# A gated cross-attention and ternary FFN block on one core: FFN tiles kept in PSUM, quads interleaved, softmax division moved

## The reference

```
x = x + tanh(g_xattn) * attention(k=ctx, v=ctx, q=layernorm(x))      # one head of 512, softmax over 722
x = x + tanh(g_ffn)   * ffn(layernorm(x))

ffn(x): h = bit_linear(x, w1)                 # 512 -> 2048
        h = depthwise_conv1d(h) along the 100 rows, 3 taps, with bias
        h = silu(h)
        return bit_linear(h, w2)              # 2048 -> 512
bit_linear(x, w): x to int8 by the row's largest |x|, w to -1, 0 or 1 by the mean of |w|
```

## Time and profile before

| | us |
|---|---|
| median of 3 runs | 380.28 (377.44 to 380.42) |
| the profiled execution, its span | 377.6 |
| PE busy | 299.4 (79%) |
| DVE busy | 213.1 (56%) |
| ACT busy | 156.3 (41%) |
| POOL busy | 99.7 (26%) |

### The profile page before, as it was taken

One profiled execution on the slowest core, in us unless ns is written; L12 is line 12 of the kernel. 1 busy time (PEld: TensorE's weight loads), 2 busy tenths in 40 slices (PEclk: granted clock), 3 DMA queues, 4 the chain that ended last, 5 costly groups with the idle time before them and its releaser, 6 DMA issues. The chain is left out here.

```text
span 377.6 us, 4595 instructions
## 1 busy us (share of the span) xinstructions
PE 299.4 (79%) x1624; PEld 216.1 (57%) x1624; DVE 213.1 (56%) x442; ACT 156.3 (41%) x291; POOL 99.7 (26%) x132
## 2 busy tenths in 40 slices
...
GB/s 202 216 228 319 39 160 259 119 0 214 10 234 146 0 104 54 112 47 1 3 117 43 102 56 0 1 2 0 23 23 0 0 1 23 0 22 0 24 0 65
DMA packets 11312, 28.02 MB, mean 74 GB/s; under 512 B 1225, under 2 KB 1225, under 8 KB 10138
## 3 DMA queue, kind: packets, MB, share of 16 engines
...
...
## 5 line engine op out<-in xcount | busy, mean ns | idle before, releaser
L861 POOL TENSOR_TENSOR z<-a,ab 128x300 f32<-128x300 f32 (+1 forms) x48 | 33.6, 700 | 72.4 <-DVE a L1088 72.4
L576 PE MATMUL pvb<-pt,ctx 120*128 120x100 f32 (+1 forms) x384 | 50.8, 294 | 1.8 <-ACT pt L747 1.8
L576 PEld LDWEIGHTS pvb<-pt,ctx 120*128 120x128 f32 (+1 forms) x384 | 49.4, 209 | 3.6 <-issue 3.5
L642 PE MATMUL ff<-xqt,w1t 128*128 128x300 bf16 (+1 forms) x192 | 35.0, 333 | 15.2 <-DVE u L1081 12.9
L555 PE MATMUL sc<-kt,qm 128*100 128x361 f32 x128 | 42.0, 478 | 0.0
L808 ACT ACTIVATE a<-u,convb,conv 128x300 f32<-128x300 f32 (+1 forms) x48 | 28.7, 598 | 17.9 <-DVE u L1081 17.9
L642 PEld LDWEIGHTS ff<-xqt,w1t 128*128 128x128 bf16 x192 | 20.0, 115 | 28.1 <-DVE u L1081 20.1
L872 POOL TENSOR_SCALAR zq<-z_i 128x300 bf16<-128x300 int8 (+1 forms) x48 | 25.9, 567 | 36.2 <-DVE z_i L1126 36.2
L536 PE MATMUL tr<-ident,ctx 120*128 120x120 f32 (+1 forms) x192 | 31.0, 285 | 2.6 <-ACT kt L726 2.2
L1088 DVE SCALAR_TENSOR_TENSOR a<-u,conv,a 128x297 f32<-128x297 f32 (+1 forms) x48 | 27.6, 574 | 8.9 <-ACT a L808 8.3
L555 PEld LDWEIGHTS sc<-kt,qm 128*100 128x100 f32 x128 | 21.3, 172 | 15.7 <-issue 1.4
...
## 6 DMA issues: line engine op xcount, KB each, us to landing
...
```

The source lines that it names most:

```text
L576: mm = nc.tensor.matmul(pvb[:, k * S:(k + 1) * S], cx[b % NCTX][0:r, i, k * P:(k + 1) * P], pt[0:r, i, :], start=(i == 0), stop=(i == 5))
L642: mm = nc.tensor.matmul(ffb[j % 2][:, 0:w], w1t[:, k, j * P:(j + 1) * P], xqt[:, k, 0:w], start=(k == 0), stop=(k == DK - 1))
L861: nc.gpsimd.tensor_tensor(z[:, j - 1, 0:w].rearrange("p (b s) -> p b s", b=nb), a1[:, n % NBUF, 0:w].rearrange("p (b s) -> p b s", b=nb), ...
```

## The change

It has three parts. First, u goes back into the tile's own PSUM bank, the `u` buffers are gone, ACT and y1 read the bank, and PE's claim of the bank waits for y1 (`y1_ok`), where it waited for u (`u_ok`). y1 now waits for `ab` too. POOL adds in place in `a1`, and silu reads `a1`. Second, silu writes `z` as [quad, column, tile of the quad], so that the four values which the maximum compares lie side by side. `quant` takes a quad at once on DVE and on POOL (4 steps, where there were 16), and `f2` waits for quads. Third, the probabilities are no longer divided: `norm` makes a [100x1] product of reciprocal and gate, and `res` multiplies y by it. `pt` no longer waits for `norm`. `FILL_CUTS` is adapted to the fewer quant steps.

```diff
@@ -66,7 +66,7 @@
 OUT_LAG = 3
 KT_LATE = 2
-FILL_CUTS = [28, 36, 50, 67, 88, 105, 117, 134]
+FILL_CUTS = [28, 36, 50, 67, 76, 93, 104, 122]
 def allowed(step, out, since):
...
@@ -131,7 +131,7 @@
         return out + [("rbc", g), ("xqt", g, b1 - 1)]
     def qz(g):
-        return [("am1", g), ("am2", g)] + [("quant", g, j) for j in range(NJ)]
+        return [("am1", g), ("am2", g)] + [("quant", g, q) for q in range(NQ)]
     def ff_f2(g, bs):
...
@@ -265,20 +265,20 @@
-        z_i8 = at(o_at + 9600 + D * 4 + 2 * NJ * GW, "z_i8", [P, NI8, GW], I8)
+        z_i8 = at(o_at + 9600 + D * 4 + 2 * NJ * GW, "z_i8", [P, 2, GW, QUAD], I8)
-        z_at = region(max(z_bytes + (3 * NBUF + 4) * t_bytes + 4 * NBUF * GW // S + 16, CHUNK * CW * 4 + CW))
-        z = at(z_at, "z", [P, NJ, GW], F32)
-        u = at(z_at + z_bytes, "u", [P, NBUF, GW], F32)
+        z_at = region(max(z_bytes + (2 * NBUF + 4) * t_bytes + 4 * NBUF * GW // S + 16, CHUNK * CW * 4 + CW))
+        z = at(z_at, "z", [P, NQ, GW, QUAD], F32)
...
@@ -557,8 +558,8 @@
                     mm.then_inc(sc_ps, 1)
                 elif kind == "pt":
                     b = step[1]
                     claim("sc", pt_ok, 2 * (b + 1))
-                    pe.wait_ge(norm_ok, b + 1)
                     for n, i in enumerate((0, 1, 3, 4)):
                         nc.tensor.transpose(sc[0:TS, 0, n * S:(n + 1) * S],
                                             probs[:, tile_start(i):tile_start(i) + TS], ident[0:S, 0:S])
...
@@ -634,7 +635,8 @@
                     if j >= NJ:
                         continue
                     w = cols(g)
-                    claim(f"ff{j % 2}", u_ok, NJ * g + j + 1)
+                    claim(f"ff{j % 2}", y1_ok, NJ * g + j + 1)
                     if j == 0:
                         pe.wait_ge(xqt_ok, GROUPS[g][1])
                         pe.wait_ge(wt_ok, 2 * CHUNK)
...
@@ -660,7 +662,7 @@
                     pe.wait_ge(wt_ok, 4 * CHUNK)
                     for j in range(NJ):
                         if bs[0] == GROUPS[g][0]:
-                            pe.wait_ge(hq_ok, NJ * g + j + 1)
+                            pe.wait_ge(hq_ok, NQ * g + j // QUAD + 1)
                         for b in bs:
                             i = b - GROUPS[g][0]
                             mm = nc.tensor.matmul(f2_bank(g, b)[0][0:S, :], zq[:, j, i * S:(i + 1) * S], w2t[:, j, :],
...
@@ -804,16 +806,20 @@
                         act.wait_ge(u_ok, n + 1)
                         if n >= NBUF:
-                            act.wait_ge(pre_ok, n - NBUF + 1)
-                        nc.scalar.activation(a1[:, n % NBUF, 0:w], u[:, n % NBUF, 0:w], ACT.Identity,
+                            act.wait_ge(z_ok, n - NBUF + 1)
+                        u = ffb[j % 2][:, 0:w]
+                        nc.scalar.activation(a1[:, n % NBUF, 0:w], u, ACT.Identity,
                                              bias=convb[:, j:j + 1], scale=conv[:, j, 1:2]).then_inc(a1_ok, 1)
-                        nc.scalar.activation(ab[:, n % NBUF, 0:nb, 0:S],
-                                             u[:, n % NBUF, 0:w].rearrange("p (b s) -> p b s", b=nb), ACT.Copy,
+                        nc.scalar.activation(ab[:, n % NBUF, 0:nb, 0:S], u.rearrange("p (b s) -> p b s", b=nb), ACT.Copy,
                                              scale=conv[:, j, 2:3]).then_inc(ab_ok, 1)
                     if 2 <= j < NJ + 2:
                         n = NJ * g + j - 2
                         act.wait_ge(pre_ok, n + 1)
-                        nc.scalar.activation(z[:, j - 2, 0:w], z[:, j - 2, 0:w], ACT.Silu).then_inc(z_ok, 1)
+                        q, i = (j - 2) // QUAD, (j - 2) % QUAD
+                        if g and i == 0:
+                            act.wait_ge(zi_ok, NQ * (g - 1) + q + 1)
+                        nc.scalar.activation(z[:, q, 0:w, i], a1[:, n % NBUF, 0:w], ACT.Silu).then_inc(z_ok, 1)
         @block.gpsimd
         def _(pool):
...
@@ -855,21 +861,18 @@
                         n = NJ * g + j - 1
                         pool.wait_ge(y1_ok, n + 1)
                         pool.wait_ge(ab_ok, n + 1)
-                        if g:
-                            pool.wait_ge(zi_ok, NJ * (g - 1) + j)
-                        nc.gpsimd.tensor_tensor(z[:, j - 1, 0:w].rearrange("p (b s) -> p b s", b=nb),
-                                                a1[:, n % NBUF, 0:w].rearrange("p (b s) -> p b s", b=nb),
-                                                ab[:, n % NBUF, 0:nb, 1:S + 1], ALU.add).then_inc(pre_ok, 1)
+                        a = a1[:, n % NBUF, 0:w].rearrange("p (b s) -> p b s", b=nb)
+                        nc.gpsimd.tensor_tensor(a, a, ab[:, n % NBUF, 0:nb, 1:S + 1], ALU.add).then_inc(pre_ok, 1)
                 elif kind == "quant":
-                    _, g, j = step
+                    _, g, q = step
                     w = cols(g)
-                    n = NJ * g + j
+                    n = NQ * g + q
                     pool.wait_ge(zi_ok, n + 1)
-                    if g and j == 0:
+                    if g and q == 0:
                         pool.wait_ge(f2_ps, GROUPS[g][0])
-                    nc.gpsimd.tensor_scalar(zq[:, j, 0:w], z_i8[:, n % NI8, 0:w], 1.0, 0.0,
+                    nc.gpsimd.tensor_scalar(zq[:, QUAD * q:QUAD * (q + 1), 0:w],
+                                            z_i8[:, n % 2, 0:w, :].rearrange("p s i -> p i s"), 1.0, 0.0,
                                             ALU.mult, ALU.add).then_inc(hq_ok, 1)
         @block.vector
...
@@ -986,9 +989,12 @@
                 elif kind == "norm":
                     b = step[1]
                     dve.wait_ge(exp_ok, b + 1)
+                    if b == 0:
+                        dve.wait_ge(gates_ok, 1)
                     link(nc.vector.reciprocal(einv[:, b:b + 1], esum[:, b:b + 1]))
-                    nc.vector.tensor_scalar(probs[:, :], probs[:, :], einv[:, b:b + 1], None,
-                                            ALU.mult).then_inc(norm_ok, 1)
+                    nc.vector.tensor_tensor(y_gate[:, b:b + 1], einv[:, b:b + 1], gates[0:S, 0:1],
+                                            ALU.mult).then_inc(y_gate_ok, 1)
                 elif kind == "pv":
                     _, b, k = step
                     if k < DK - 1:
...
@@ -1001,7 +1007,8 @@
                     b = step[1]
                     dve.wait_ge(y_ps, b + 1)
                     dve.wait_ge(xb_ok, b + 1)
-                    nc.vector.scalar_tensor_tensor(x_sb[:, b, :], yb[0:S, :], gates[0:S, 0:1], x_sb[:, b, :],
+                    dve.wait_ge(y_gate_ok, b + 1)
+                    nc.vector.scalar_tensor_tensor(x_sb[:, b, :], yb[0:S, :], y_gate[:, b:b + 1], x_sb[:, b, :],
                                                    ALU.mult, ALU.add).then_inc(x2_ok, 1)
                     dve.wait_ge(x2_ok, b + 1)
                     link(nc.vector.bn_stats(stats[:, b, :], x_sb[:, b, :]))
...
@@ -1074,24 +1081,22 @@
                     if j < NJ:
                         n = NJ * g + j
                         dve.wait_ge(ff_ps, n + 1)
-                        if n >= NBUF:
-                            dve.wait_ge(ab_ok, n - NBUF + 1)
-                            dve.wait_ge(y1_ok, n - NBUF + 1)
-                        nc.vector.tensor_tensor(u[:, n % NBUF, 0:w], ffb[j % 2][:, 0:w], row_wide[:, 0:w],
-                                                ALU.mult).then_inc(u_ok, 1)
+                        u = ffb[j % 2][:, 0:w]
+                        nc.vector.tensor_tensor(u, u, row_wide[:, 0:w], ALU.mult).then_inc(u_ok, 1)
                     if 1 <= j < NJ + 1:
                         n = NJ * g + j - 1
                         dve.wait_ge(a1_ok, n + 1)
+                        dve.wait_ge(ab_ok, n + 1)
                         a = a1[:, n % NBUF, 0:w].rearrange("p (b s) -> p b s", b=nb)[:, :, 1:S]
-                        v = u[:, n % NBUF, 0:w].rearrange("p (b s) -> p b s", b=nb)[:, :, 0:S - 1]
+                        v = ffb[(j - 1) % 2][:, 0:w].rearrange("p (b s) -> p b s", b=nb)[:, :, 0:S - 1]
                         nc.vector.scalar_tensor_tensor(a, v, conv[:, j - 1, 0:1], a, ALU.mult, ALU.add).then_inc(y1_ok, 1)
                     if j >= 3 and (j - 3) % QUAD == QUAD - 1:
                         q = (j - 3) // QUAD
                         dve.wait_ge(z_ok, NJ * g + j - 2)
-                        nc.vector.tensor_reduce(acc_q[:, q % 2, 0:w], z[:, q * QUAD:(q + 1) * QUAD, 0:w].rearrange("p j s -> p s j"),
-                                                AX.X, ALU.max, apply_absolute_value=True).then_inc(acc_q_ok, 1)
+                        nc.vector.tensor_reduce(acc_q[:, q % 2, 0:w], z[:, q, 0:w, :], AX.X, ALU.max,
+                                                apply_absolute_value=True).then_inc(acc_q_ok, 1)
                         if q:
                             n = NJ // QUAD * g + q + 1
...
@@ -1117,13 +1122,14 @@
```

(13 more changed lines are left out.)

13 lines of the change are left out of this document (7 added, 6 removed).

## The result

| | before | after |
|---|---|---|
| median of four runs, us | 380.04 (377.44 to 380.42) | 410.78 (408.25 to 412.81) |
| ratio after / before, 95% interval | | 1.0849 [1.0788, 1.0910] |
| span of the profiled execution, us | 377.6 | 408.4 |
| first u to last maximum, groups 0, 1, 2, us | 25.4, 32.5, 32.0 | 31.9, 44.6, 43.5 |
| last group: first quantisation to the output additions, us | 12.9 | 17.0 |

The direction was forecast (0.88 for slower), the size was not: 400 was named with a range of 388 to 408, and the time is 410.8. VectorE is busy for 22 us less and the kernel takes 31 us more.

A forecast was written before the change was run, and what follows sets the result against it. The FFN stages were taken as chains of waits, with no engine full. Terms of 3 (group 0), 6 (group 1), 8.5 (group 2) and 2 (last quantisation) made 19.5 us on 380.3: 400 us, range 388 to 408.

The forecast's parts named there:

- The ring: FFN stages: y1(j-1), tile j+1 on PE, u(j+1), y1(j) in sequence, 1.68 us a tile, 2.16 at the lower clock.
- clock term of the FFN stages: Group 2's FFN stage: +5.0 at full clock, +13 at the lower; taken at +8.5 us.
- full-clock sum: Group 2's FFN stage added up step by step with PE at full clock: 37.0 us against 32.0, +5.0.
- Group 1: Its FFN stage, net of `scores` work moved ahead: +5.1 us at full clock, +11.9 at the lower; taken at +6.
- Group 0: Its FFN stage, with 200 columns: +1.6 to +4.8 us; taken at +3.
- Quantisation at the end: Last stage: a whole quad passes DVE, then POOL, before PE's first matmul; +1.4 to +3.7 us, taken at +2.
- silu term left at nothing: FFN stages on ACT: no extra time was counted for silu's scattered writes.
- second sign of being wrong: FFN stages: the forecast is wrong if silu's scattered writes make ACT need more than 1.68 us a tile.
- Softmax at nothing: Attention: dropping the division's 6.5 us of DVE gains 0, since y and context transposes hide it.
- quad maximum at 1.37 us: FFN stages on DVE: the contiguous read cuts it from 2.21 to 1.37 us, four times a stage.
- PSUM at nothing: u and y1 on DVE: access to PSUM costs 0, with ends of -0.05 and +0.1 an instruction.
- the clock falls in every FFN stage: Rival, all lower-clock ends: 33 us more, 413 us; half the excess gives 406; chance 0.17 (405 and above).

The follow-up runs named there:

- experiment 1: The changed kernel with u back in its SBUF buffers and the PSUM bank given back at u: 384.58 us, ratio to before 1.0199.
- experiment 2: The kernel before with only u moved to PSUM, the bank held until y1: 409.50 us, ratio to before 1.0867.
- experiment 3: The changed kernel with the last group's FFN tiles rotating over four PSUM banks: 397.01 us, ratio to before 1.0531.
- experiment 4: The changed kernel with three extra unused matmuls behind each FFN tile but three of the last group: 404.80 us, ratio to before 1.0730.
- Experiment 7: The changed kernel with POOL's conversion to bf16 issued by tile, not by quad: 406.36 us, ratio to before 1.0784.
- experiment 5: The kernel before with only the softmax change, probabilities left undivided: 378.52 us, ratio to before 1.0012.

## Why the prediction was right in its mechanism and wrong in its size

- **The ring** was right, by its own numbers: 1.68 us at full clock and 2.16 at the lower, measured 1.69 and 2.18. A turn with a maximum in it was put at 2.6 and is 2.64. Experiments 1, 2 and 3 show that it makes nearly all of the longer stages: without it 1.5, 2.9 and 1.4 us are left.
- **The failed step is the clock term of the FFN stages**, as in "I take +8.5: the stage starts on the lower clock already, and its `f2` bring the clock back". They do, but for three tiles each. In group 2 eight ring tiles ran at the lower clock. One of them (360.72) cost nothing, since DVE was at its maximum: u to u is 2.64 us there, as in experiment 4 at full clock. The other seven cost 0.49 each, 3.4. The two steps with an `f2` in them, put at 4.0, are 3.97 in experiment 4 and 5.07 and 5.88 here: 3.0 more. So the clock took 6.4 us, where I gave it 3.5. With the +5.0 of the full-clock sum that is 11.4, measured 11.6.
- **Group 1**, taken at +6 between 5.1 and 11.9, came to +9.5. PE's timeline has 7 tiles at about 1.18 us there, 6 of them on the path, and an `f2` of 5.04 us: 2.9 + 1.4 over 5.1 is 9.4. The same error. That it comes out so close is partly luck: the stage is 1.3 us longer than this sum has it, and the `scores` steps behind it gave back 2.6, where I counted 1.3.
- **Group 0**, taken at +3, came to +6.5, above its lower-clock end of +4.8. All its ring tiles but the last ran at the lower clock (0.85 us each, 1.64 a ring, 1.6 forecast). The two PV parts among them took 2.77 and 1.81 us, where my end left them at their old 1.5 each; that is nearly all of the 1.7 above the end. Experiment 7's 29.4 us for the same instructions, +4.0, shows that the stage moves by more than 2 us with the clock alone.
- **Quantisation at the end**, taken at +2 between 1.4 and 3.7, came to +4.05. Of this 2.62 is the later first matmul: DVE's quad took 1.41, at its lower end, but POOL's first took 2.28 beside DVE's second, near its upper end. 7 more matmuls at the lower clock, 0.21 each, are 1.5, and this term had no clock in it. That part isn't firm: in experiments 3 and 4 the same instructions came to +2.7 and +2.5.
- **The silu term left at nothing** was wrong in itself, and hidden. ScalarE needs 1.71 us a tile, just above the ring at full clock and under it at the lower. That is the prediction's own second sign of being wrong, and it came true without being the cause. It shows only where the ring is cut: 1.5 to 2.9 us a stage in experiment 1. The wait of `a1` for silu was in no term either.
- **Softmax at nothing** (experiment 5) and **the quad maximum at 1.37 us** (1.395) were right.
- **PSUM at nothing** was right: u takes 0.48 there for 0.46, y1 0.52 for 0.53, and ScalarE's `a1` 0.60 for 0.62. The 65 ns more for y1, worked out from the Trainium skill ("Perfetto Trace Analysis", Optimizing Scalar/DVE Operations), don't appear in this trace; the measurement decides.
- **The rival** "the clock falls in every FFN stage" is what happened. Its full price was 413 us, 33 us of terms against 30.8 us of span measured. I halved its excess to 406 and closed the range at 408, so the range left out the case's own worked-out price. The rule named beside it, the Trainium skill's "TensorE: Matmul & The Clock Gate" (A second HAM failure mode: psum-queue depth-cycling), is borne out by this trace: short idles before each group of matmuls, a clock of 0.63 to 0.81, and by experiment 4, which won 4.4 us by filling the idles.

**Open:** why the clock is regained for just three tiles, why group 0 ran at 0.63, 0.68 or 0.72 in kernels that have the same ring, and how ScalarE's 0.40 us more a tile divides between silu's write and the wait.
